# A two-layer graph network kernel: constants converted by ScalarE, weights loaded later, variances by six VectorE operations, and a piece of the third group's sums issued earlier

## The reference, cut to what matters

```python
edge_index = jnp.stack([src, dst])                       # 53125 edges, sorted by dst, 3125 nodes of 128 features
h = jnp.maximum(_layernorm(x, axis=-1), 0.0)
x = x + _L0_gnn_ref(h, edge_index, W_in, b_in, W1, b1, W2, b2, clearance)
h = jnp.maximum(_layernorm(x, axis=-1), 0.0)
x = x + _L1_gnn_ref(h, edge_index, G1, gb1, G2, gb2)     # two graph convolutions

def _L0_gnn_ref(...):
    h = jnp.tanh(gat_out @ W_in + b_in)
    def step(h, _):                                      # 12 steps
        agg = segment_sum(h[src], dst) / deg
        diff = jnp.tanh(gelu(agg @ W1 + b1) @ W2 + b2)
        return h + (diff - relu(clearance) * h) * 0.5, None
```

## Time and profile before

| what | value |
|---|---|
| median of 3 runs | 1267.23 us (1266.03 to 1267.9) |
| the profiled execution's own time | 1266.38 us |
| its span, first to last instruction | 1264.8 us |
| TensorE busy | 1227.2 us (97%) |
| VectorE busy | 411.5 us (33%) |
| ScalarE busy | 306.4 us (24%) |
| GpSimd busy | 570.8 us (45%) |
| mean granted TensorE clock | 0.989 |

### The profile page before, as it was taken

One profiled execution on the slowest core, in us unless ns is written; L12 is line 12 of the kernel. 1 busy time (PEld: TensorE's weight loads), 2 busy tenths in 40 slices (PEclk: granted clock), 3 DMA queues, 4 the chain that ended last, 5 costly groups with the idle time before them and its releaser, 6 DMA issues.

```text
span 1264.8 us, 17221 instructions
## 1 busy us (share of the span) xinstructions
PE 1227.2 (97%) x6757; PEld 695.0 (55%) x6757; DVE 411.5 (33%) x853; ACT 306.4 (24%) x455; POOL 570.8 (45%) x426
## 2 busy tenths in 40 slices
PE   3899999999999999999999999999999999999998
PEld 1776565564564655645556456455564564555645
DVE  7999323131130231311302214113122142382412
ACT  1898222130131221301312113113131131130100
POOL 6700104827718448277284481772845818600000
PEclk8799999999999999999999999999999999999999
DMA  4000211222222312222222222231222223420101
GB/s 103 3 1 1 66 34 37 36 56 40 35 59 35 56 38 35 58 36 34 60 35 54 40 35 59 35 47 47 36 52 42 35 58 67 92 62 1 52 17 35
DMA packets 106136, 54.58 MB, mean 43 GB/s; under 512 B 13238, under 2 KB 104473, under 8 KB 105964
## 3 DMA queue, kind: packets, MB, share of 16 engines
q0 software_dynamic: 46352, 23.46, 14.4%
q1 hardware_dynamic: 57958, 29.48, 8.7%
q10 hardware_dynamic: 1782, 1.06, 0.3%
HBM read 32.53 MB, written 21.04 MB: 42 GB/s over the span
## 4 chain that ended last, share of the span: by engine, by line
PE 91%; DVE 6%; issue 1%; DMA 1%; ACT 1%; POOL 0%; DVEq 0%; ACTq 0%; POOLq 0%
PE ps L907 63%; PE ps L971 11%; PE ps L961 10%; PE ps L812 4%; DVE scratch L1447 3%; PE ps L795 2%; PE ps L1082 1%; PE ps L950 1%; DMA adj<-packed_scratch,adj 1%; DVE adj L1301 0%; DVE state L1730 0%; DVE lo L1430 0%; DVE cols L1351 0%; DVE adj L1392 0%; ACT adj L1174 0%
## 5 line engine op out<-in xcount | busy, mean ns | idle before, releaser
L907 PE MATMUL ps<-adj,hi 128*128 128x512 f16 (+2 forms) x2000 | 710.7, 367 | 0.0
L907 PE MATMUL ps<-adj,lo 128*128 128x512 f16 (+2 forms) x1920 | 693.8, 367 | 0.0
L684 POOL DMA_INDIRECT scratch<-state_scratch,tail_rows x264 | 390.6, 1480 | 390.4 <-DMA state_scratch<-state 313.2
L907 PEld LDWEIGHTS ps<-adj,hi 128*128 128x128 f16 x2000 | 194.3, 97 | 218.1 <-issue 12.9
L907 PEld LDWEIGHTS ps<-adj,lo 128*128 128x128 f16 x1920 | 186.8, 97 | 213.2 <-issue 14.6
L1622 DVE TENSOR_TENSOR ps<-ps,bias 128x512 f32<-128x512 f32 (+2 forms) x84 | 53.8, 641 | 488.9 <-PE ps L971 488.9
L1219 ACT ACTIVATE scratch<-ps 128x512 f32<-128x512 f32 (+2 forms) x84 | 46.3, 552 | 574.3 <-DVE ps L1622 573.3
L1210 ACT ACTIVATE scratch<-ps,b1c,cols 128x512 f32<-128x512 f32 (+2 forms) x156 | 107.3, 740 | 176.9 <-PE ps L961 176.1
L971 PEld LDWEIGHTS ps<-w,scratch 128*128 128x128 f32 (+1 forms) x1152 | 138.4, 190 | 14.0 <-issue 5.3
L971 PE MATMUL ps<-w,scratch 128*128 128x128 f32 (+1 forms) x1152 | 143.6, 276 | 0.1
L684 POOL DMA_INDIRECT entry<-state_scratch,tail_rows x88 | 129.7, 1474 | 26.8 <-issue 26.8
(11 more groups left out here) (218 smaller groups left out, 420.3 us busy)
## 6 DMA issues: line engine op xcount, KB each, us to landing
state_scratch<-state SPq DMA_DIRECT2D x55, 256.0 KB, 2.3
scratch<-state_scratch,tail_rows POOLq DMA_INDIRECT x264
state_scratch<-state SPq DMA_DIRECT2D x11, 192.0 KB, 2.0
scratch<-rdeg_scratch SPq DMA_DIRECT2D x1, 1562.5 KB, 8.8
entry<-state_scratch,tail_rows POOLq DMA_INDIRECT x88
state<-in_x_dram SPq DMA_DIRECT2D x5, 256.0 KB
scratch<-in_x_dram SPq DMA_DIRECT2D x5, 256.0 KB
x_scratch<-state SPq DMA_DIRECT2D x5, 256.0 KB, 3.7
```

Of the source, the lines that this page charges most:

```text
L684: nc.gpsimd.indirect_dma_start(tail_sum[i], None, state_dram, bass.IndirectOffsetOnAxis(ap=tail_rows[:, at:at + 1], axis=0), compute_op=AL ...
L907: return nc.tensor.matmul(bank, values[:, k, :], adj[:, k, c0:c0 + n], start=is_first, stop=is_last)
```

## The change

Five edits in one:

1. GpSimd makes the counts once each in 32 bits (`count_lf`, `count_rf`, ahead of `s_const`) instead of twice each in 16 bits behind it. ScalarE converts and repeats them.
2. The eight weight DMAs of ScalarE move from behind the packed edges to behind the eviction of batch 1.
3. The 25 `bn_aggr` and one operation become six operations on the 25 tiles at once (five, and the last one that was there in another form); the doubled mean is halved in `norm_factors`.
4. TensorE's small product with `tail_order` and the twelve last tiles of the third group's sums (24 matmuls) move ahead of the flag's load and the wait for the last eviction, behind a new wait for the eviction of batch 51.
5. `EARLY_PARTS` for the path that is taken when an edge was missed covers the third group whole; this path isn't run on these inputs.

```diff
-EARLY_PARTS = [(0, FULL - 1), (0, FULL), (0, EARLY_LATE - FULL)]
+EARLY_PARTS = [(0, FULL - 1), (0, FULL), (0, FULL)]
...
+        count_lf = hid[:, 0, 0:P]
+        count_rf = hid[:, 0, P:P + WROW]
...
             nc.gpsimd.iota(chunk_d[:, CHUNK + 1:CHUNK + 2], pattern=[[0, 1]], base=0, channel_multiplier=CHUNK, **big)
+            nc.gpsimd.iota(count_lf, pattern=[[1, P]], base=0, channel_multiplier=0, **big)
+            nc.gpsimd.iota(count_rf.rearrange("p (k d) -> p k d", d=WIN), pattern=[[1, TILES], [LANES, WIN]], base=1,
+                           channel_multiplier=0, **big)
             nc.gpsimd.iota(wfirst, pattern=[[WQ * WIN, WCOLS]], base=0, channel_multiplier=WIN, **big).then_inc(s_const, 1)
-            nc.gpsimd.iota(count_l, pattern=[[1, 128], [0, RUN]], base=0, channel_multiplier=0, **big)
-            nc.gpsimd.iota(count_r.rearrange("p (k d) w -> p k d w", d=WIN), pattern=[[1, TILES], [LANES, WIN], [0, RUN]],
-                           base=1, channel_multiplier=0, **big).then_inc(s_counts, 1)
...
             window(0, 0, ps[:, 0, :], 0).then_inc(s_last[1], 1)
+            pe.wait_ge(s_ev[1], BATCHES // 2 + OPEN)
+            nc.tensor.matmul(ps[0:SET_NODES, 5, 0:SETS], tail_order, tail_blocks, start=True, stop=True
+                             ).then_inc(s_boff, 1)
+            first_sums(2, (EARLY_LATE - FULL, FULL))
...
-                nc.tensor.matmul(ps[0:SET_NODES, 5, 0:SETS], tail_order, tail_blocks, start=True, stop=True
-                                 ).then_inc(s_boff, 1)
-                first_sums(2, (EARLY_PARTS[2][1], FULL))
                 pe.wait_ge(s_owner, 1)
...
-            act.wait_ge(s_packed_out, 48)
-            act.dma_start(w1[:, :], W1).then_inc(s_w, 16)
...
+            act.wait_ge(s_const, 1)
+            for counts, values, n in ((count_l, count_lf, P), (count_r, count_rf, WROW)):
+                last = nc.scalar.activation(counts, values.rearrange("p (n o) -> p n o", o=1).broadcast_to((P, n, RUN)), ACT.Copy)
+            last.then_inc(s_counts, 1)
...
             for b in range(ENTRY_BATCHES):
                 evict(b % 2, b // 2)
+                if b == 1:
+                    load_weights()
...
             def variances():
-                for k in range(TILES):
-                    last_ = V.bn_aggr(mv[:, k, :], stats[:, k, :])
-                link(last_)
-                return V.tensor_scalar(ln_b[:, :], mv[:, :, 1], EPS, None, ALU.add)
+                mean_e, mean_o, dev_e, dev_o = (stats[:, :, i] for i in (1, 4, 2, 5))
+                V.tensor_tensor(mv[:, :, 0], mean_e, mean_o, ALU.add)
+                V.tensor_tensor(ln_b[:, :], dev_e, dev_o, ALU.add)
+                link(V.tensor_tensor(ln_a[:, :], mean_e, mean_o, ALU.subtract))
+                link(V.scalar_tensor_tensor(out=ln_a[:, :], in0=ln_a[:, :], scalar=FEAT / 4, in1=ln_a[:, :], op0=ALU.mult,
+                                            op1=ALU.mult))
+                link(V.tensor_tensor(ln_b[:, :], ln_b[:, :], ln_a[:, :], ALU.add))
+                return V.tensor_scalar(ln_b[:, :], ln_b[:, :], 1 / FEAT, EPS, ALU.mult, ALU.add)
```

More of the change, by code:

```diff
@@ L1120, in _, with load_weights @@
                 act.dma_start(b_entry[p:p + 1, :], b_in.rearrange("(a f) -> a f", a=1)).then_inc(s_b_in, 16)
-            act.wait_ge(s_packed_out, 48)
-            act.dma_start(w1[:, :], W1).then_inc(s_w, 16)
[L1123 to L1130, removed]
+            act.wait_ge(s_const, 1)
+            for counts, values, n in ((count_l, count_lf, P), (count_r, count_rf, WROW)):
+                last = nc.scalar.activation(counts, values.rearrange("p (n o) -> p n o", o=1).broadcast_to((P, n, RUN)), ACT.Copy)
+            last.then_inc(s_counts, 1)
+            def load_weights():
+                act.dma_start(w1[:, :], W1).then_inc(s_w, 16)
+                act.dma_start(w2[:, :, :], W2.rearrange("(h p) f -> p h f", p=FEAT)).then_inc(s_w, 16)
+                act.dma_start(wg[:, 0, :], G1).then_inc(s_w, 16)
+                act.dma_start(wg[:, 1, :], G2).then_inc(s_w, 16)
+                for i, b in enumerate((b2, gb1, gb2)):
+                    act.dma_start(bias[:, i, :], b.rearrange("(a f) -> a f", a=1).broadcast_to((P, FEAT))
+                                  ).then_inc(s_w, 16)
+                with nc.allow_non_contiguous_dma("a bias of 256 as two columns"):
+                    act.dma_start(b1c[:, :], b1.rearrange("(h p) -> p h", p=FEAT)).then_inc(s_w, 16)
             def slot_edges(g):
@@ L1417, in norm_factors @@
                 link(V.reciprocal(ln_a[:, :], ln_a[:, :]))
-                V.scalar_tensor_tensor(out=ln_b[:, :], in0=mv[:, :, 0], scalar=-1.0, in1=ln_a[:, :], op0=ALU.mult,
+                V.scalar_tensor_tensor(out=ln_b[:, :], in0=mv[:, :, 0], scalar=-0.5, in1=ln_a[:, :], op0=ALU.mult,
                                        op1=ALU.mult).then_inc(s_ln, 1)
```

## The result

The changed kernel takes **1270.15 us** (median of 16 runs, 1268.67 to 1272.8), the kernel before on the same chip 1266.99 (16 runs, 1265.7 to 1269.98): ratio 1.0026, 95% interval 1.0018 to 1.0033. It is slower by 0.26%; faster by 5 us was forecast. The profiled execution took 1269.38 us, its span is 1267.8 us, the mean granted clock 0.988. The span is 3.0 us longer than before's.

The account below looks back on a forecast made before the run. TensorE's products over `adj` bound everything behind the setup; the change acts in the first 134 us, mostly VectorE's chain. Keys 3.9, variances 0.9, weights 0 and third group 0.2 sum to 5.0 us: 1262.2 us, range 1260.8 to 1265.0.

Parts of the forecast that it names:

- the third group's rest: TensorE's 24 matmuls restart behind batch 51's eviction, not the last one: gain 0.2 us, bounds 0.25 and -0.8.
- the start: Until the edge packing: line 1301 shortens, packing starts at 5.2 instead of 6.71 us: gain 1.5 us, bounds 1.7 and 0.7.
- The first gather: Ahead of `key_group`: issued at 11.0, landed by 16.0 without weights beside it; keys 3.9 us earlier, 1.5 from the start.
- Variances: VectorE ahead of the first one-hots: six operations take 0.95 us instead of 1.89, gain 0.9 us.
- Weights among evictions: ScalarE's eight weight issues behind batch 1's eviction: cost taken as 0, upper price 1.2 us.
- B: ScalarE's weight issues stall its evictions by 1.2 us: gain 3.8 us, 1263.4 us; chance 0.20.
- C: x rows, not weights, slow the first gather, which lands at 18.7: gain 3.3 us, 1263.9 us; chance 0.10.
- D: VectorE's line 1301 takes its 3.49 us whatever GpSimd does: gain 3.2 us, 1264.0 us; chance 0.08.
- E: VectorE's earlier start meets another wait in the first batches: under 2.5 us left, 1265.5 us; chance 0.08.
- F: TensorE's clock stays low for more early batches, losing 7.5 us: slower, above 1269.8 us; chance 0.04.

Follow-up runs that it names:

- e1: Changed kernel with the flag's load and branch ahead of the small product and 24 matmuls, and the skipped path as short as before's: 1262.07 us.
- e4: Kernel before with edits 1 to 3 alone, TensorE's order and skipped path as before: 1262.24 us.
- e11: e1 with the 16-bit counts made by GpSimd again behind the constants, no conversion on ScalarE: 1262.92 us.
- e9: e1 with the weight loads back at the start, behind the packed stores and ahead of the conversions: 1264.24 us.
- e12: Kernel before with only the skipped path made 48 matmuls longer, 24 longer than e7's; nothing executed changed: 1271.41 us.
- e2: Changed kernel, branch still late, with only the skipped path as short as before's: 1262.70 us.
- e7: Kernel before with only the skipped path made 24 matmuls longer: 1267.17 us.
- e8: Changed kernel with the skipped path 12 matmuls longer than before's, half of edit 5: 1268.34 us.
- e5: Kernel before with edits 4 and 5 only, the new TensorE order and the longer skipped path: 1273.88 us.
- e3: Changed kernel with the broadcast load and the copy of the short tile held until TensorE's owners' product: 1267.59 us.
- e14: e8 with the broadcast and the copy held until the owners' product, as in e3: 1267.37 us.

## Why the prediction was wrong

**The step that failed** is the third group's rest: "the cover is the queue of matmuls; if there is none, it costs about 1 us", with bounds 0.25 and -0.8. The load and the branch were priced by their durations in the earlier trace rows and by before's own branch, as if these were properties of the instructions. The load nearly kept its price (0.70 us against 0.50). The branch took 7.65 instead of 0.37, 4.85 of it uncovered by 24 matmuls, and 2.1 us more went at the lower clock: about -7 in place of +0.2. The branch's length was taken from the one kernel in which its target had been fetched; edit 4 moved it 25 rows down the code, edit 5 put 24 more into the path it skips, and the prediction counted both at nothing because they don't execute.

**The sum without it was right.** 5.0 us were forecast, and e1 gives 4.7 of them; without the 0.2 of edit 4 it is 4.8, and e4 gives 4.55. In its terms: the start, 1.5 forecast, was 1.05, because the edges themselves land near 5 us and their conversions (5.05 to 5.66) stand ahead of the packing; the forecast had allowed 0.2 for a completion and nothing for these. Line 1301's 3.49 us go with GpSimd's long counts: they are there in before and e11 and 0.17 without them. It ended behind the second of the two counts, not between them, so how they hold it isn't shown. The first gather was issued at 12.02, not 11.0, and that term was misread in the rows of before: there the search's result is ready at 12.09 and the gather starts at 13.14, 1.05 us later. The forecast put this down to the bias terms and took 0.4 for the issue. In the changed kernel the terms are done at 10.21, the result is ready at 10.96, and it is 1.06 again. Neither reached the keys in this trace, since the gather landed early enough: 4.0 us there against 3.9. Variances 0.89 against 0.9. Weights among evictions nothing at the end, as forecast: e9, without them there, is slower than e1 by the gather's wait and not faster. The reason given holds in part: the issues run ahead of the eviction of batch 1, but that of batch 2 waits for them where TensorE's product is there early.

**The rivals.** B (the issues stall ScalarE, since they begin only behind batch 1's eviction) fell by the row at 31.98; the 1.39 us of idle time ahead of batch 2's eviction are what is true of it. C (the x rows slow the gather, and the completion rule quoted with it) fell by e9: the x rows are there in both, and only the place of the weights differs between e9 and e1, 2.2 us; the rule's effect does not show in this gather. D fell: 0.17 us. E fell: 4.7 us reach the end in e1. F (slower) named the low clock in the batches, and a piece of it came: the batches that took 6.47 us before (44.34 to 50.81) took 8.37 (39.32 to 47.69), since the clock was at 0.50 until 45.5; some 0.7 us were given back later, and the lead went from 5.01 to 3.84. In e1 the last full eviction starts at 127.59, 4.73 us earlier than before's: this part of the loss isn't in every kernel with that start. That left a kernel faster by 4. The slower outcome came from a mechanism that no rival had: the fetch of code.

## What to carry to other kernels

A taken branch is priced by where its target lies, not by its duration in another version of the code: code that never executes cost 4.2 us in e12 and, beside the broadcast, over 7 (after against e2), when it pushed the target over the edge of what has been fetched. Look at the instruction queue's packets before moving a branch, keep skipped paths short, and put the branch, and what follows it within one packet, ahead of a burst of DMA traffic, not behind it. Where an edit consists of parts, time them apart: here 4.7 us of gain (e1: 1262.07, the best version) and 8 of loss (1270.15 against e1) came as one.

## What the runs showed of the hardware that was not expected

- TensorE's code comes in packets of 16 KB on its own queue, some 250 instructions each. A fetch takes 3.3 us from the start of the branch to its end on idle DMA engines, and up to 7.6 beside a 1.6 MB broadcast and a 0.4 MB copy; with those two under way the packet started 5 us after the branch instead of 1.0.
- The place of the target decides, not the distance: e7 skips as much code as the changed kernel and shows no stall.
- The stall has two faces: a long branch when the target is beyond the edge (e12, after), or a gap ascribed to issue in straight code behind a short branch (e8, 4.3 us), since the next packet is asked for only at the branch (it starts 1.1 us after the branch does in before, e1, e4 and e7).
- A standstill of 4 to 5 us brought the granted clock to 0.50, and it stayed there for 3 to 6 us of full work behind it (140.5 to 143.3 in e8, 140.4 to 144.5 in the changed kernel, 136.6 to 141.6 in e12, 143.7 to 150.1 in e5). The 2.9 us of e3 and e14 did the same, for 3.4 us.
- ScalarE's sequencer issued a DMA 0.98 us ahead of the start of the eviction that stands before it in the code (31.98 against 32.96).
